# A decoder layer's second weights, routing order, last norm and beginning, rearranged

## The reference

```
x   = norm(x + mix(x))             # mix: phase memories by cumulative sums, gates, a norm, and @ Wo
x   = norm(x + cross(x, context))  # 16 heads, 1601 context rows, softmax over the queries' axis
x   = norm(x + experts(x))         # router picks 2 of 8 experts per token; each is relu(x W1 + b1) W2 + b2

mix:  pos = (cos p * cumsum(cos p * v) + sin p * cumsum(sin p * v)) / 16,   v = x Wpv + bpv
      kv  = the same with phase tanh(x Wk + bk) * pi, values x Wkv and a gate sigmoid(gelu([x, shifted x] Wg1) Wg2)
      blend of the two by a softmax of two, norm with gain ln_g and bias ln_b, @ Wo + bo
norm(x) = (x - mean) / sqrt(var + 1e-5)
```

## Time and profile before

| what | us |
|---|---|
| median of 3 runs (lowest, highest) | 2271.31 (2265.58, 2274.38) |
| the profiled execution's own time | 2271.26 |
| its span, first to last instruction | 2269.6 |
| PE busy | 1993.4 |
| DVE busy | 1754.7 |
| ACT busy | 1548.2 |
| POOL busy | 727.7 |

### The profile page before, as it was taken

One profiled execution on the slowest core, in us unless ns is written; L12 is line 12 of the kernel. 1 busy time (PEld: TensorE's weight loads), 2 busy tenths in 40 slices (PEclk: granted clock), 3 DMA queues, 4 the chain that ended last, 5 costly groups with the idle time before them and its releaser, 6 DMA issues. The chain is left out here.

```text
span 2269.6 us, 43525 instructions
## 1 busy us (share of the span) xinstructions
PE 1993.4 (88%) x10630; PEld 1048.6 (46%) x10638; DVE 1754.7 (77%) x3559; ACT 1548.2 (68%) x4361; POOL 727.7 (32%) x967
## 2 busy tenths in 40 slices
PE   6999898499999999999999998887637999999993
PEld 2454455223222232222322221113536999999993
DVE  4989885399999999999999999996444555555554
ACT  3565565399999999999999999996212333333334
POOL 0112112044444434444344441110553333333331
PEclk9989999699999999999999999999868999999997
DMA  4111104846675665766667666652751222222224
GB/s 151 42 42 70 56 24 139 166 80 105 129 132 109 125 103 128 131 113 129 97 132 126 115 118 86 117 68 81 220 131 29 35 37 37 36 36 37 35 37 160
DMA packets 126117, 212.39 MB, mean 94 GB/s; under 512 B 31554, under 2 KB 94786, under 8 KB 124882
## 3 DMA queue, kind: packets, MB, share of 16 engines
q1 hardware_dynamic: 98272, 151.74, 36.6%
q0 software_dynamic: 26240, 59.00, 9.9%
q10 hardware_dynamic: 1554, 1.05, 0.2%
HBM read 138.38 MB, written 73.74 MB: 93 GB/s over the span
## 5 line engine op out<-in xcount | busy, mean ns | idle before, releaser
L1400 ACT ACTIVATE w_all<-psum,neg_max 128x512 f32<-128x512 f32 (+1 forms) x1664 | 1111.4, 737 | 46.3 <-DVE neg_max L1308 44.4
L1308 DVE TENSOR_REDUCE neg_max<-psum 128x1 f32<-128x512 f32 (+1 forms) x1664 | 1025.3, 676 | 18.5 <-PE psum L1245 14.9
L1245 PE MATMUL psum<-qst,kst 96*128 96x512 bf16 (+1 forms) x1664 | 530.3, 391 | 98.2 <-ACT w_all L1400 61.0
L1213 PE MATMUL psum<-w_all 128*32 128x512 f32 (+1 forms) x3328 | 450.5, 615 | 9.8 <-DVE w_all L1322 9.8
L1245 PEld LDWEIGHTS psum<-qst,kst 96*128 96x128 bf16 (+1 forms) x1664 | 130.0, 98 | 686.9 <-ACT w_all L1400 641.3
L1400 ACT ACTIVATION_READ_ACCUMULATOR w_all<-psum,neg_max 128x1 f32 (+1 forms) x1664 | 428.3, 257 | 0.0
L1734 ACT ACTIVATE hid<-psum,b 128x128 f32<-128x128 f32 x568 | 161.9, 368 | 378.3 <-PE psum L1679 374.0
L1372 POOL TENSOR_TENSOR w_all<-vst,inv 128x64 f32<-128x64 f32 (+1 forms) x416 | 121.0, 291 | 687.5 <-DVE inv L1276 686.7
L1679 PE MATMUL psum<-xst,w 128*128 128x128 f32 x2272 | 267.9, 277 | 0.0
L1679 PEld LDWEIGHTS psum<-xst,w 128*128 128x128 f32 x2272 | 262.0, 194 | 0.1
L1689 PE MATMUL psum<-area,hid 128*128 128x256 f32 x1136 | 256.9, 379 | 0.0
(11 more groups left out here) (208 smaller groups left out, 1885.2 us busy)
## 6 DMA issues: line engine op xcount, KB each, us to landing
kst<-k_parts SPq DMA_DIRECT2D x384, 112.0 KB, 6.5
k_parts<-k_out POOLq DMA_DIRECT2D x52, 336.0 KB, 3.2
w_all<-in_W SPq DMA_DIRECT2D x16, 1024.0 KB
area<-in_ctxT SPq DMA_DIRECT2D x16, 896.0 KB, 4.7
vst<-v_all SPq DMA_DIRECT2D x64, 224.0 KB, 9.2
qst<-q_parts SPq DMA_DIRECT2D x192, 64.0 KB, 5.9
v_all<-area POOLq DMA_DIRECT2D x13, 896.0 KB, 4.3
q_parts<-q_out POOLq DMA_DIRECT2D x24, 256.0 KB, 3.0
```

Source lines behind the costliest of these rows:

```text
L1213: last = pe.matmul(psum[j * PAD:(j + 1) * PAD, 6, :], v_scaled[0:r, pb, j, :], probs_at[pb][0:r, j, :], start=t == 0, stop=t == ST - 1)
L1245: pe.matmul(psum[0:r, 2 * sbuf + i, :], kst[:, h, j, t * P:t * P + r], qst[:, h, j, :], start=True, stop=True).then_inc(scores_ready, 1)
L1308: v.tensor_reduce(neg_max[0:r, sbuf, i:i + 1], psum[0:r, 2 * sbuf + i], AX_X, ALU.min) \
L1400: act.activation(probs_at[pb][0:r, j, :], psum[0:r, 2 * sbuf + i, :], ACT.Exp, bias=neg_max[0:r, sbuf, i:i + 1], scale=-1.0, accum_out=sum ...
```

## The change

Six things are done.

1. `weights` holds cols, the first sequence's xT, Wpv and Wk; the rest is `more_weights`, with a semaphore of its own. The first sequence's x is loaded behind them. PE projects Wpv first and waits for `more_loaded` after Wk.
2. DVE does its passes over the positions first, and ACT the sines and cosines before everything else, with a table load of their own.
3. Scaling `wo_c` (`scale_wo`) goes into step 0 of DVE behind the first scans, and `centre_wo` behind the gate's sum. PE makes the means in bank 0, after ACT has read it, and waits for `wo_ready` only before `keys(1)`.
4. In block 3 SP loads W2 of experts 1 to 7 and then b2 behind the stores of the last rows, and DVE reads the three first lists before it waits for them and copies tile 0's weights.
5. PE's `ranks(c - 2)` comes behind `turn(c - 1)` and `project(c + 1, (0, 1))`.
6. In the last norm ACT does two of the four operations of a sequence and POOL the other two, as `tensor_scalar` with two pointers. SP waits for both.

Two pairs of semaphores are merged besides.

```diff
             weights = [
                 (cols[:], a["cols"]),
+                (xt[:, 0, :, 1:L + 1], a["xT"][0]),
+                (wpv[:], a["Wpv"].rearrange("(c p) d -> p c d", p=P)),
                 (wk[:], a["Wk"].rearrange("(c p) d -> p c d", p=P)),
+            ]
+            more_weights = [
                 (wg1[:], a["Wg1"].rearrange("(c p) d -> p c d", p=P)),
...
-                    load(0, 0)
+                    sp.sem_inc(xt_loaded[0], 16)
                     for tile, src in weights:
                         sp.dma_start(tile, src).then_inc(weights_loaded, 16)
+                    for tile, src in more_weights:
+                        sp.dma_start(tile, src).then_inc(more_loaded, 16)
+                    sp.dma_start(xin[:, 0].rearrange("p t d -> p (t d)"), a["x"][0]).then_inc(xt_loaded[0], 16)
                     load(1, 1)
...
-                        if not (isinstance(b, int) and b == 0):
-                            wait(pe, q_split, PARTS * (b - 1))
+                        if isinstance(b, int) and b == 1:
+                            pe.wait_ge(wo_ready, 1)
+                        else:
+                            pe.wait_ge(q_split, PARTS * (b - 1))
                         project(0, wk, now(h), C).then_inc(kz_ready, 1)
...
-                    pe.wait_ge(xt_loaded[0], 32)
+                    project(5, wpv, now(0), C).then_inc(pv_ready, 1)
                     project(0, wk, now(0), C).then_inc(kz_ready, 1)
+                    pe.wait_ge(more_loaded, 16 * len(more_weights))
                     project(2, wg1, now(0), 2 * C).then_inc(gh_ready, 1)
                     blend(0, 0)
-                    project(5, wpv, now(0), C).then_inc(pv_ready, 1)
-
+
+                    pe.wait_ge(phase_ready, 1)
                     pe.wait_ge(derived_ready, 1)
+                    pe.wait_ge(wo_scaled, 1)
                     for k in range(C):
-                        pe.matmul(psum[:, 7, 0:D], mean_w[:], wo_c[:, k, :], start=k == 0, stop=k == C - 1)
+                        pe.matmul(psum[:, 0, 0:D], mean_w[:], wo_c[:, k, :], start=k == 0, stop=k == C - 1)
...
                     gates(0, 0)
-                    pe.wait_ge(wo_ready, 1)
                     blend_weights(0, 0)
...
+                    act.preload_act_table_set("trig_and_small")
+                    act.wait_ge(consts_made, 1)
+                    act.wait_ge(pos_ready, 1)
+                    act.activation(pos_sin[:], pos[:], ACT.Sin)
+                    act.activation(pos_cos[:], turns[:], ACT.Sin, bias=half_pi[:], scale=-1.0).then_inc(trig_ready, 1)
+                    act.preload_act_table_set("gelu_and_others")
                     act.wait_ge(weights_loaded, 16 * len(weights))
...
+                    def scale_wo():
+                        v.wait_ge(more_loaded, 16 * len(more_weights))
+                        for k in range(C):
+                            last = v.tensor_scalar(wo_c[:, k, :], wo[:, k, :], col(LNG + k), None, ALU.mult)
+                        last.then_inc(wo_scaled, 1)
+
+                    def centre_wo():
+                        v.wait_ge(wo_mean_ready, 1)
+                        v.wait_ge(consts_loaded, N_CONSTS)
+                        for k in range(C):
+                            v.tensor_tensor(wo_c[:, k, :], wo_c[:, k, :], psum[:, 0, 0:D], ALU.subtract)
+                        v.tensor_tensor(bo_half[:], rows[:, BO, :], psum[:, 0, D:2 * D], ALU.add).then_inc(wo_ready, 1)
+                        v.wait_ge(wo_ready, 1)
+                        v.tensor_scalar(bo_half[:], bo_half[:], 0.5, None, ALU.mult).then_inc(wo_ready, 1)
...
-            W2_IN_STEP = {3: (1,), 4: (2,), 5: (3,), 6: (4, 5), 7: (6, 7)}
...
-                        for e in W2_IN_STEP.get(c, ()):
-                            load_w2(sp, e)
...
+                    for c in range(B):
+                        route_step(c)
+                    for e in range(W2_EARLY, E):
+                        load_w2(sp, e)
                     sp.dma_start(b2_all[:], a["b2"].rearrange("(o e) d -> o e d", o=1).to_broadcast([P, E, D])) \
                         .then_inc(b2_loaded, 16)
-                    for c in range(B):
-                        route_step(c)
...
                     for b in range(B):
                         sp.wait_ge(out_ready, b + 1)
+                        sp.wait_ge(out_rest_ready, REST + b + 1)
                         sp.dma_start(out[b], y3(b)).then_inc(out_stored, 16)
...
+                    for b in range(B):
+                        pool.wait_ge(y3_loaded[b], 16)
+                        pool.wait_ge(rstd3_ready, b + 1)
+                        pool.wait_ge(shift2_ready, B + b + 1)
+                        for t in range(TT // 2, TT):
+                            at = y3(b)[:, t * D:(t + 1) * D]
+                            last = pool.tensor_scalar(at, at, rstd3[:, b, t:t + 1], shift3[:, b, t:t + 1],
+                                                      ALU.mult, ALU.add)
+                        last.then_inc(out_rest_ready, 1)
...
                     def route_step(c):
-                        if 0 <= c - 2 < B:
-                            ranks(c - 2)
                         if 0 <= c - 1 < B:
                             turn(c - 1)
                         if c + 1 < B:
                             project(c + 1, (0, 1))
+                        if 0 <= c - 2 < B:
+                            ranks(c - 2)
                         if 0 <= c - 1 < B:
                             route(c - 1)
...
-                        for t in range(TT):
+                        act.wait_ge(shift2_ready, B + b + 1)
+                        for t in range(TT // 2):
...
-                    v.wait_ge(ffn_loaded, 32 * E)
                     opened(v, y_scaled)
                     v.sem_inc(y_scaled, 1)
-                    at = copy_weights(slice(0, 1), 0)
                     for d in range(3):
                         name_rows(d, 16)
+                    v.wait_ge(ffn_loaded, 32 * E)
+                    at = copy_weights(slice(0, 1), 0)
```

More of the change, by code:

```diff
@@ L888, in _ @@
                 def _(v):
+                    v.wait_ge(pos_loaded, 16)
+                    v.tensor_scalar(turns[:], pos[:], 1.0 / TWO_PI, ROUND, ALU.mult, ALU.add).then_inc(dve_pos, 1)
+                    v.wait_ge(dve_pos, 1)
+                    v.tensor_scalar(turns[:], turns[:], -ROUND, None, ALU.add).then_inc(dve_pos, 1)
+                    v.wait_ge(dve_pos, 2)
+                    v.scalar_tensor_tensor(pos[:], turns[:], -TWO_PI_HI, pos[:], ALU.mult, ALU.add).then_inc(dve_pos, 1)
+                    v.wait_ge(dve_pos, 3)
+                    v.scalar_tensor_tensor(pos[:], turns[:], TWO_PI_HI - TWO_PI, pos[:], ALU.mult, ALU.add) \
+                        .then_inc(dve_pos, 1)
+                    v.wait_ge(dve_pos, 4)
+                    v.tensor_scalar(pos[:], pos[:], -PI_DOWN, PI_DOWN, ALU.max, ALU.min).then_inc(dve_pos, 1)
+                    v.wait_ge(dve_pos, 5)
+                    v.scalar_tensor_tensor(turns[:], pos[:], -1.0, pos[:], ALU.mult, ALU.max).then_inc(pos_ready, 1)
                     v.wait_ge(weights_loaded, 16 * len(weights))
@@ L902, in _ @@
                         v.tensor_copy(lnb_wide[:, k, :], col(LNB + k).to_broadcast([P, P]))
-                        v.tensor_scalar(wo_c[:, k, :], wo[:, k, :], col(LNG + k), None, ALU.mult)
-                    v.wait_ge(dve_pos, 1)
+                    v.wait_ge(dve_pos, 6)
                     v.tensor_copy(wb2_wide[:], mcols[:, 1:2].to_broadcast([P, P])).then_inc(derived_ready, 1)
-                    v.wait_ge(pos_loaded, 16)
-                    v.tensor_scalar(turns[:], pos[:], 1.0 / TWO_PI, ROUND, ALU.mult, ALU.add).then_inc(dve_pos, 1)
@@ L916, in _ @@
-                    v.wait_ge(dve_pos, 5)
-                    v.tensor_scalar(pos[:], pos[:], -PI_DOWN, PI_DOWN, ALU.max, ALU.min).then_inc(dve_pos, 1)
-                    v.wait_ge(dve_pos, 6)
-                    v.scalar_tensor_tensor(turns[:], pos[:], -1.0, pos[:], ALU.mult, ALU.max).then_inc(pos_ready, 1)
-                    v.wait_ge(wo_mean_ready, 1)
-                    v.wait_ge(consts_loaded, N_CONSTS)
-                    for k in range(C):
-                        v.tensor_tensor(wo_c[:, k, :], wo_c[:, k, :], psum[:, 7, 0:D], ALU.subtract)
@@ L926, in _ @@
-                    v.tensor_tensor(bo_half[:], rows[:, BO, :], psum[:, 7, D:2 * D], ALU.add).then_inc(wo_ready, 1)
-                    v.wait_ge(wo_ready, 1)
-                    v.tensor_scalar(bo_half[:], bo_half[:], 0.5, None, ALU.mult).then_inc(wo_ready, 1)
-                    v.wait_ge(trig_ready, 1)
+                    v.wait_ge(trig_ready, 1)
+                    def scale_wo():
[3 more added lines that the diff above has]
+                        last.then_inc(wo_scaled, 1)
@@ L1001, in step @@
                             last.then_inc(moments_ready, 1)
-                        if not end or mix:
-                            pass
```

(4 more changed lines are left out.)

35 lines of the change are left out of this document (11 added, 24 removed).

## The result

The changed kernel takes 2257.01 us in the median (2256.01 to 2260.53), before 2271.32: the ratio is 0.9943 with a 95% interval of 0.992 to 0.9965. It is faster, by 14 us where I had forecast 32, and outside my range of 2222 to 2255. Its profiled execution took 2257.59 us (span 2255.9), 13.7 less than that of before.

| stretch | predicted | measured |
|---|---|---|
| start to `kvg` (L1027, now L1045) | -13.7 | 51.23 to 39.17: -12.1 |
| `kvg` to block 3's first `norm_rows` | 0 | 1527.1 to 1532.3: +5.2 |
| that to the first list copy | -15.6 | 132.3 to 129.8: -2.5 |
| first list copy to the last loads' statistics | +1.9 | 533.4 to 533.2: -0.2 |
| last norm, first statistics to the end | -4.5 | 25.6 to 21.5: -4.1 |

A forecast was written before the change was run, and what follows sets the result against it. Three quarters of the time was taken as one-engine-bound and untouched (attention by ScalarE and VectorE, expert tiles by PE). 2271.3 - 13.7 (beginning) - 13.7 (routing) - 4.5 (last norm) = 2239.4 us; 8-in-10 range 2222 to 2255.

The forecast's parts named there:

- (a): Routing: four W2 copies taken out of the steps save 2.9 us each, so the last rows come 11.6 us earlier.
- the last rows no earlier relative to the routing's start: Routing: named sign that the forecast is wrong, with 2251 us as the total then expected.
- (c) to (e): Routing, last rows to first list copy: slots(7) at 1680.3, scatters done 1695.0, W2 copies done 1694.4; list copy 15.6 us earlier.
- passengers: Rival, routing: W2 only rode along in the waits, last rows stay at 1671.5, total 2250.9 us; chance 16%.
- (b): Routing: `turn` ahead of `ranks` saves 4.1 us at turn(7), nothing in earlier steps.
- The tie: Routing's end: W2 copies ending at 1694.4 and scatters allowing the list copy at 1695.0; first list copy taken as 1695.
- (f): After the first list copy: `copy_weights` of tile 0 behind the list reads delays `take_rows(0)` by 1.9 us.
- The beginning: Start to `kvg`: PE starts near 10.1 and `kvg` at 37.5 instead of 51.23, 13.7 us gained and kept until attention.
- The last norm: Last norm: VectorE's statistics at 1.84 us become the pace, POOL operations take 0.76 us; gain 4.5 us.
- Its own range 2231 to 2248: Total: the forecast's own range in us, given for a beginning of 11 to 15 and last norm to -2.6.
- waits gone: Rival, routing: without W2 no wait is left and POOL works through, 26.3 us instead of 13.7, total 2226.8; chance 20%.

The follow-up runs named there:

- b_w2: Kernel before with item 4 alone (W2 and b2 behind the last rows' stores, lists read ahead of the wait for weights): 2273.52 us, ratio 1.0019.
- x_scat_last: Changed kernel with W2 in the steps and no scatter before all eight sequences have their slots: 2288.61 us, one run.
- a_best_2: a_best once more, on chip D: 2249.98 us, ratio 0.9926 to the kernel before.
- a_ranks_first_2: a_best with `ranks` ahead of `turn` again, as in the kernel before, on chip D: 2249.90 us, ratio 0.9923.
- after_again: The changed kernel run again unedited, on chip B: 2258.86 us, ratio 0.9958 to the kernel before.
- a_fill: Changed kernel plus six extra PE matmuls of 128x512 in the idle time ahead of `turn`, result unchanged: 2261.76 us, ratio 0.9964 to the kernel before.
- a_best: Changed kernel with W2 in the steps, b2 ahead of step 0 and tile 0's weights copied before the list reads, as before: 2249.98 us, ratio 0.9915.
- a_w2_in_steps: Changed kernel with W2 in the steps and b2 ahead of step 0 as before, new read order kept: 2250.92 us, ratio 0.991 to the kernel before.
- a_six_2: a_best with six of each sequence's eight scatters in the steps and two at the end, on chip D: 2256.47 us, ratio 0.9947.
- a_ranks_first: a_best with `ranks` ahead of `turn` again, on chip C: 2232.48 us, ratio 0.992 to the kernel before on that chip.

## Why the prediction was wrong, point by point

**The step that failed** is (a) of the routing, that of the W2 copies taken out of the steps four "are worth 1.05 / 0.362 = 2.9 us each, 11.6 in all". The rows came 2.3 us earlier after block 3's start (93.1 to 90.8), not 11.6. The copies are worth nothing that these profiles show: the last rows come after 90.6 us without them in the steps (b_w2) and after 89.4 and 93.1 with them, and in x_scat_last all seven stand in the steps and the rows take 66.4 us. The prediction had named this sign of being wrong itself: "the last rows no earlier relative to the routing's start". W2 was a passenger in time that was lost anyway. I had the row that says so, the wait that began before the first W2 copy was issued, and read "may lengthen it" out of a window of three microseconds in which W2 passed at the full rate. What passes at the full rate during a wait has not been shown to cause it. By the Trainium skill's rule on queues (DMA: Bandwidth & Descriptors, Queues, rings and completion order) a removed copy was worth next to nothing, and here the trace agrees: 90.6 against 89.4 and 93.1 us. That holds for the rows; what the copies did to the scatters stands under (c) to (e). The rival "passengers" (16%, 2250.9) had this mechanism right.

In the terms of the forecast the way to the first list copy measures: the last rows -2.3 (forecast -11.6), from them to the last slots -3.3 (-4.1), to the last scatter's issue -1.0 (0), landing +4.0 (0), in sum -2.5 instead of -15.6.

**(b) The turn's 4.1 us** do not show in the totals: the medians of a_best_2 and a_ranks_first_2 differ by 0.1 us, and with six runs of each that is known to some 3 us either way. In the changed kernel the time from the last rows to the last slots did fall, 24.5 to 21.3 us, and on chip D it is 22.6 us with `turn` first and 24.3 with `ranks` first; what gives the difference back in the totals is not shown.

**(c) to (e) The tie** between scatters and copies. I had the copies end at 1694.4 after 33.9 us; they were issued from 1663.11 and ended near 1700, after 37. And I had set the cost of a tie at nothing. What I left out: the scatters themselves land late beside copies. Landing took 8.2, 11.7, 9.1 and 10.5 us in the four profiles with W2 behind the rows (changed, after_again, b_w2, a_fill) and 4.2 to 5.1 in those with W2 in the steps and the full result, but for x_scat_last with 6.2. The view of the DMA queues shows it: packets of q0, the queue on which the scatters' small packets run, that were still to move when POOL's last scatter had ended, in the changed kernel (1694 to 1701.3 us) and before (1707.4 to 1710.7):

```profile
q0 software_dynamic: 136, 0.00, 1.4%
```

```profile
q0 software_dynamic: 32, 0.00, 0.8%
```

That makes item 4, W2 and the order of the reads together, a loss of some 4 us on the kernel before (b_w2), and of 9 us on the changed kernel (2258.86 against a_best's 2249.98, on one chip). In these last two profiles 6.4 of the 10.1 us lie between the start of block 3 and the first list copy, 1.2 behind it, and 2.4 in blocks 1 and 2, which item 4 does not touch. No rival of mine had the late landing.

**(f)** `copy_weights` after the reads: from the first list copy to PE's first tile 8.77 us instead of 7.49, so +1.3 for my +1.9. In these two profiles most of it is given back within the first tile; between a_w2_in_steps and a_best it is not (534.0 and 532.7 us from the first list copy to the last loads' statistics).

**The beginning** was -12.1 where I had -13.7: PE starts at 11.05, not 10.1, and needs 28.1 us until `kv` is read, not 27.2. That is 1.6 us of the total; the larger miss, 5.2 us, lies behind `kvg`. The sentence that failed is "Steps follow one another by VectorE, so the gain stays until attention starts". A step is 41.2 us if `turn` and the twenty matmuls behind it have the full clock, and about 44 if they have not. That they then stand in ScalarE's and VectorE's way is my reading of the order of the work. PE, after (timeline; the number in brackets is the idle time before):

```profile
76.00 1.94 PE L539 MATMUL psum<-ident,w_all 128*128 128x128 f32 x8 [4.45 <-ACT w_all L817]
77.73 10.53 PE L468 MATMUL psum<-w_all 128*128 128x512 f32 x20
...
119.85 1.06 PE L539 MATMUL psum<-ident,w_all 128*128 128x128 f32 x8 [1.45 <-ACT w_all L817]
120.75 8.75 PE L468 MATMUL psum<-w_all 128*128 128x512 f32 x20
...
161.08 1.94 PE L539 MATMUL psum<-ident,w_all 128*128 128x128 f32 x8 [4.79 <-ACT w_all L817]
162.82 10.66 PE L468 MATMUL psum<-w_all 128*128 128x512 f32 x20
```

and two windows of it (granted clock third from the end), one where the half clock (1.2 GHz) lies ahead of the idle time and is absorbed by it, one where it lies on `turn`:

```profile
108.00:114.00 6.00, 6.00 (x21) 4.10 (x21) 2.93 (x8) 4.72 (x10) 0.00 (x0) 0.55 0.00 0
...
161.00:168.00 7.00, 6.92 (x16) 4.02 (x17) 6.93 (x5) 2.12 (x3) 4.05 (x3) 0.60 0.05 19
```

The last `turn` of block 1 starts at 339.03 us before and at 332.66 after, so of the 12.1 us 6.4 are left there. From `kvg` to block 3 the three profiles with the old beginning (one long step each) need 1527.1 us. With the new one five need 1528.2 to 1529.2 us (two long steps, in a_six_2 with a lesser third), and seven with three need 1530.9 to 1532.3. x_scat_last, with two, needs 1525.4; its difference lies behind block 1, since from the last `turn` to block 3 it needs 1235.6 us and all others 1238.6 to 1239.4, and its cause is open. So mostly 1 to 5 of the 12 us are lost again, and the loss goes with where the half clock falls. Why it falls there more often with the new beginning isn't shown.

**The last norm** was right: VectorE's 1.84 us is the pace, and only the POOL operation was cheaper (0.56, not 0.76 us); 4.1 us for 4.5.

**The range.** "Its own range 2231 to 2248" does not follow from the bounds it names: a beginning of 15 us and a last norm of 4.9 give together 2238, and a beginning of 11 with a last norm of -2.6 gives 2249. The measured 2257 lies above either.

**What would have been wrong in the other direction.** The rival "waits gone" has its case too: on chip C, where no release is late, the list of a_ranks_first comes after 105.0 us and on chip D, with late releases, after 128.6. If nothing else of block 3 differs between the chips, the waits are worth 23.6 of the 29.2 us that I had counted; W2 just isn't what makes them.

**What stays open**: how a scatter holds back a release of PE, and why not on chip C. Shown on chips B and D, with one profile of each: none with no scatter or four a sequence beside the steps, 14.2 us with six, 21 to 33 with eight. Not shown: whether it is their number or that they follow without a pause, and what in PE's path they share. The record has one more hint and one more limit. In before all five late releases come 1.2 to 2.5 us after POOL has ended a run of eight or sixteen scatters (the first: 1617.08, then `logits` at 1618.32); in the changed kernel only one of the three of `logits` does, the other two come while POOL scatters. And on chip C a_ranks_first issues all 64 scatters without a pause and has no late release, so scatters in a row are not enough by themselves.

## What to carry to other kernels

A copy that runs during a wait can have caused it only if the wait starts after the copy; look at when each was issued before pricing its removal. Moving bulk loads behind the last stores puts them beside whatever small scatters or loads the next stage waits for, so price their landing, not only the queue's total. A step "bound by one engine" can still have a chain through the others that decides in some steps: compare the pitch of all steps before passing a gain on.

## What the runs showed of the hardware

- A release of PE arrived 15.1 us after its matmuls had ended (1637.85 to 1652.97), while PE itself went on until 1641.54. On chips A, B and D such waits appear in every profile where POOL issues six or eight indirect DMAs a sequence beside PE's work, and in none of the two with four or none; in three profiles on chip C there is none. The kernel before is 19 us (0.8%) faster there.
- In block 1 of the changed kernel PE is granted half the clock for one stretch of some 7 us in nearly each step of 41 us, and the same in a_fill in 150 to 156 us, with PE busy throughout (0.53); filling the idle time left fewer such stretches, but not none.
- Scatters of 128 x 8 bytes have landed 4.2 to 5.1 us after the last issue where W2 had been sent before (6.2 in x_scat_last), and 8.2 to 11.7 us beside copies at 190 to 280 GB/s.
- A POOL operation with two operators and two pointers takes 560 ns for 256 float32 elements a partition, against 1327 ns for 448 in the earlier trace rows, where it has one operator and writes bfloat16.
